# Two convolutions with group normalization: singles of both convolutions side by side, both roots taken ahead of mid's normalization, and a new order of VectorE's work

## The reference

```python
x = x + _L0_conv_ref(_gn(x), L0_conv_weight, L0_conv_threshold)   # 3x3, padding 1, weights masked by a threshold
x = x + _L1_conv_ref(_gn(x), L1_conv_kernel, L1_conv_bias)        # 5x5 by FFT, which is a 5x5 convolution with padding 2, plus bias

def _gn(v, G=16, eps=1e-05):          # groups of 2 channels over the whole image
    g = v.reshape(B_, G, C_ // G, H_, W_)
    m = jnp.mean(g, axis=(2, 3, 4), keepdims=True)
    s = jnp.var(g, axis=(2, 3, 4), keepdims=True)
    return ((g - m) / jnp.sqrt(s + eps)).reshape(v.shape)
```

## Time and profile before

| | |
|---|---|
| median of 3 executions | 901.29 us (901.25 to 901.67) |
| the profiled execution | 901.0 us, of which its span is 899.2 us |
| mean granted TensorE clock | 0.955 |
| busy: PE, PE weight loads, DVE, ACT, POOL | 88%, 57%, 68%, 37%, 26% of the span |
| DMA | 150.59 MB, mean 167 GB/s |

### The profile page before, as it was taken

The page is one execution under the profiler, slowest core; times in us unless marked ns, Lnnn a source line. Parts: engine busy times, 40 slices in busy tenths (PEclk is TensorE's granted clock), DMA queues, the critical chain, the costliest instruction groups (busy, mean ns, idle before and its releaser), DMA issues.

```text
span 899.2 us, 67768 instructions
## 1 busy us (share of the span) xinstructions
PE 794.9 (88%) x32302; PEld 508.1 (57%) x32302; DVE 611.0 (68%) x949; ACT 336.1 (37%) x289; POOL 234.5 (26%) x165
## 2 busy tenths in 40 slices
PE   0785698989899898989899898989899898997895
PEld 0342365656567565756566575656566565664463
DVE  6676398786767697676767687686767585664141
ACT  0342234353524244353524244353524244352320
POOL 1014042322303232321303232321303232333031
PEclk9887999999999999999999999999999999999898
DMA  8989875978788686878888676978886554664313
GB/s 182 207 178 227 172 154 141 210 171 204 182 191 209 156 181 161 192 181 194 189 196 197 148 186 163 210 181 192 191 197 163 131 134 113 148 156 97 72 47 93
DMA packets 234118, 150.59 MB, mean 167 GB/s; under 512 B 18592, under 2 KB 227552, under 8 KB 229984
## 3 DMA queue, kind: packets, MB, share of 16 engines
q1 hardware_dynamic: 228768, 144.67, 70.3%
q10 hardware_dynamic: 4608, 4.23, 1.9%
q0 software_dynamic: 704, 1.25, 0.6%
HBM read 75.60 MB, written 33.59 MB: 121 GB/s over the span
## 4 chain that ended last, share of the span: by engine, by line
PE 75%; DVE 8%; issue 7%; ACT 4%; DVEq 2%; DMA 1%; POOL 1%; SPq 1%; ACTq 0%; POOLq 0%
PE psum L773 56%; PE psum L791 19%; ACT x_hi L379 3%; DVE mid L651 2%; DVEq L654 2%; DMA x_bands<-x_dram 1%; DVE bn_out L659 1%; DVE bn_in L560 1%; DVE x_lo L631 1%; ACT root L372 0%; SPq L251 0%; DVE x_lo L639 0%; DVE rinv L607 0%; DVE newton L609 0%; DVE newton L608 0%
## 5 line engine op out<-in xcount | busy, mean ns | idle before, releaser
L360 POOL TENSOR_TENSOR mid<-mid,conv_out 128x512 f32<-128x512 f32 x122 | 216.8, 1806 | 598.4 <-ACT conv_out L424 598.4
L773 PE MATMUL psum<-x_hi,s_hi 32*64 32x512 f16 x6656 | 211.8, 399 | 47.6 <-DVEq L654 37.8
L773 PE MATMUL psum<-x_hi,s_lo 32*64 32x512 f16 x6656 | 206.9, 391 | 1.9 <-issue 1.9
L773 PE MATMUL psum<-x_lo,s_hi 32*64 32x512 f16 x6656 | 200.7, 381 | 2.6 <-issue 2.6
L773 PEld LDWEIGHTS psum<-x_hi,s_hi 32*64 32x64 f16 x6656 | 107.1, 107 | 137.9 <-DVEq L654 44.6
L773 PEld LDWEIGHTS psum<-x_hi,s_lo 32*64 32x64 f16 x6656 | 126.9, 109 | 72.6 <-issue 16.0
L379 ACT ACTIVATE x_hi<-x_bands 128x2304 f16<-128x2304 f32 x32 | 68.0, 2126 | 265.4 <-PE psum L791 262.4
L651 DVE SCALAR_TENSOR_TENSOR mid<-psum,unscale,x_own 128x1024 f32<-128x1024 f32 x64 | 79.2, 1279 | 127.0 <-PE psum L791 126.5
L773 PEld LDWEIGHTS psum<-x_lo,s_hi 32*64 32x64 f16 x6656 | 111.7, 104 | 76.0 <-issue 13.9
L424 ACT ACTIVATE conv_out<-psum,bias,unscale 128x512 f32<-128x512 f32 x122 | 85.1, 777 | 61.4 <-PE psum L773 38.5
L639 DVE TENSOR_TENSOR x_lo<-mid_bands,x_hi 128x2560 f16<-128x2560 f32 x32 | 99.0, 3094 | 0.8 <-PE psum L773 0.5
(11 more groups left out here) (77 smaller groups left out, 267.9 us busy)
## 6 DMA issues: line engine op xcount, KB each, us to landing
x_own<-x_dram SPq DMA_DIRECT2D x128, 256.0 KB, 5.0
mid_bands<-mid SPq DMA_DIRECT2D x372, 80.0 KB, 2.1
out_dram<-mid SPq DMA_DIRECT2D x116, 256.0 KB, 5.5
x_bands<-x_dram SPq DMA_DIRECT2D x96, 288.0 KB, 6.1
x_bands<-x_dram SPq DMA_DIRECT2D x32, 272.0 KB, 6.4
mid_bands<-mid SPq DMA_DIRECT2D x124, 64.0 KB, 2.0
every_mv<-mv_scratch ACTq DMA_DIRECT2D x16, 256.0 KB, 3.7
out_dram<-mid SPq DMA_DIRECT2D x24, 128.0 KB, 2.4
```

Source lines behind the costliest of these rows:

```text
L360: nc.gpsimd.tensor_tensor(m, m, conv_out[:, b, :], ALU.add).then_inc(out_added, 1)
L773: ins = nc.tensor.matmul(psum[2 * C * J:2 * C * (J + 1), bank + i, :].rearrange("p (a w) -> p a w", a=A), w[quad(i), at:at + 2, :].rearran ...
```

## The change

TensorE: the helpers are cut anew. A whole step now does `pairs3_high` (96 pairs on `x3_hi`), `pairs3_low` (48 pairs on `x3_lo`), `pairs5_high` (320 pairs on `x5_hi`), `singles3` (96 singles on `x3_hi`, then 48 on `x3_lo`), `singles5` (80 singles on `x5_lo`, then 160 on `x5_hi`), `pairs5_low` (160 pairs on `x5_lo`). The number of products is as before. Two semaphores change: `high3_whole` is raised when `x3_hi` has been read for the last time, and `high3` waits for it instead of `c3_whole`; `a5_whole` now is raised after the last read of `x5_hi`, and `high5` waits for it instead of `b5_begun`, which is gone. `x3_lo` is now needed after 96 matmuls of a step, and the 5x5 banks and `x5_hi` after 144.

ScalarE: in even steps both roots are taken one after the other, ahead of `normalize5`.

VectorE: a whole step now does `low5`, `normalize3(s+1)`, (even steps) both `group_stats`, both `scale_of`, (odd steps) `stats_in` of halves s+3 and s+4, then `take_conv3`, `stats_out`, `aggregate`, and at the end `low3(s+1)` for the next step. In the lead the bound of the 5x5 weights (`largest`, `power_of_two`, for which POOL's split of these weights waits) is taken ahead of `take_conv3(1)` instead of after the statistics of mid, `low3(2)` stands ahead of `stats_out(0)`, and `take_conv3(2)` ahead of `mean_of(("mid", 0))`. TensorE's start of the lead becomes a block of its own, placed behind `lead_warm`, with a branch to it and one back.

```diff
--- before.py
+++ after.py
@@ -142,7 +142,7 @@
 
         c3_whole = sem("c3_whole")
         a5_whole = sem("a5_whole")
-        b5_begun = sem("b5_begun")
+        high3_whole = sem("high3_whole")
         b5_whole = sem("b5_whole")
         mean_mixed = sem("mean_mixed")
         var_mixed = sem("var_mixed")
@@ -375,7 +375,7 @@
 
                 act.wait_ge(norm1, h + 1)
                 if h:
-                    act.wait_ge(c3_whole, h)
+                    act.wait_ge(high3_whole, h)
                 nc.scalar.activation(x3_hi[:, :, 2:2 + W], x_bands[:, h % XB_SLOTS, :, :], ACT.Copy).then_inc(hi3_done, 1)
                 act.drain().then_inc(x3_hi_go, 1)
 
@@ -383,7 +383,7 @@
 
                 act.wait_ge(norm2, k + 1)
                 if k:
-                    act.wait_ge(b5_begun, k)
+                    act.wait_ge(a5_whole, k)
                 nc.scalar.activation(x5_hi[:, :, 2:2 + W], mid_bands[:, k % MB_SLOTS, :, :], ACT.Copy).then_inc(hi5_done, 1)
 
             def scale_by(which, v):
@@ -457,7 +457,8 @@
                     spread_stats(s - 1)
                 if gathered:
                     gather_stats(s - 1)
-                    take_root(gathered[0])
+                    for stat in gathered:
+                        take_root(stat)
                 if s == 0:
                     high3(1)
                     take_root(("x", 1))
@@ -477,8 +478,6 @@
                         high3(s + 1)
                     if has5(s + 1):
                         high5(s + 1 - LAG)
-                if len(gathered) > 1:
-                    take_root(gathered[1])
                 if exchanged(s) and s >= LAG:
                     spread_stats(s)
 
@@ -694,24 +693,24 @@
             low3(1)
             variance_of(("x", 1))
             scale_of(("x", 1))
-            take_conv3(1)
-            stats_out(0)
-            low3(2)
-            stats_out(1)
-            aggregate("mid", 0, mean_go)
             dve.wait_ge(w_loaded, 16 * 2 * Q)
             largest(w5, 1)
             power_of_two(1)
             nc.vector.drain().then_inc(w5_bounded, 1)
+            take_conv3(1)
+            low3(2)
+            stats_out(0)
+            stats_out(1)
+            aggregate("mid", 0, mean_go)
+            take_conv3(2)
             mean_of(("mid", 0))
-            take_conv3(2)
             variance_of(("mid", 0))
             scale_of(("mid", 0))
-
             low3(LAG)
             stats_in(4, range(BANKS))
             stats_in(5, range(BANKS))
             aggregate("x", 2, mv_ready)
+
             low5(0)
             stats_out(2)
             dve.wait_ge(mix_loaded, 16)
@@ -719,13 +718,13 @@
             group_stats(("x", 2))
             scale_of(("x", 2))
             normalize3(LAG + 1)
+            take_conv3(LAG)
             stats_in(6, range(BANKS))
-            take_conv3(LAG)
+            stats_in(7, range(BANKS))
             stats_out(LAG)
-            stats_in(7, range(BANKS))
             aggregate("mid", LAG // 2)
             aggregate("x", (LAG + 3) // 2, mv_ready)
-            stats_in(8, range(BANKS))
+            low3(LAG + 1)
 
             for s in range(LAG + 1, STEPS):
                 gathered = exchanged(s - 1)
@@ -734,20 +733,18 @@
                 low5(s - LAG)
                 if s > HALVES:
                     add_late(s - 1 - LAG)
-                if has3(s):
-                    low3(s)
+                if has3(s + 1):
+                    normalize3(s + 1)
                 if gathered:
                     dve.wait_ge(mv_in, 16 * exchange_number(s - 1))
-                    group_stats(gathered[0])
-                    scale_of(gathered[0])
-                if has3(s + 1):
-                    normalize3(s + 1)
-                if len(gathered) > 1:
-                    group_stats(gathered[1])
-                if has3(s + 5):
-                    stats_in(s + 5, range(BANKS))
-                if len(gathered) > 1:
-                    scale_of(gathered[1])
+                for stat in gathered:
+                    group_stats(stat)
+                for stat in gathered:
+                    scale_of(stat)
+                if s % 2:
+                    for h in (s + 3, s + 4):
+                        if has3(h):
+                            stats_in(h, range(BANKS))
                 if has3(s):
                     take_conv3(s)
                     stats_out(s)
@@ -755,6 +752,8 @@
                     aggregate("mid", s // 2, None if len(exchanged(s)) > 1 else mv_ready)
                     if len(exchanged(s)) > 1:
                         aggregate("x", (s + 3) // 2, mv_ready)
+                if has3(s + 1):
+                    low3(s + 1)
 
             take_late(HALVES - 1)
             add_late(HALVES - 1)
@@ -794,33 +793,39 @@
                                 start=start and dx == 0, stop=True, skip_group_check=True, tile_position=(i * C, j * C))
                 return ins
 
-            def high_image3():
+            def pairs3_high():
 
                 pe.wait_ge(bank3_go, 1)
                 pe.wait_ge(x3_hi_go, 1)
                 pairs(s3_hi, x3_hi, K3, X3_BANK, start=True, every=x3_hi_go)
                 pairs(s3_lo, x3_hi, K3, X3_BANK, every=bank3_go)
-                singles(s3_hi, x3_hi, K3, X3_BANK)
-                singles(s3_lo, x3_hi, K3, X3_BANK)
-
-            def low_image3():
+
+            def pairs3_low():
 
                 pe.wait_ge(x3_lo_go, 1)
                 pairs(s3_hi, x3_lo, K3, X3_BANK, every=x3_lo_go)
+
+            def singles3():
+
+                singles(s3_hi, x3_hi, K3, X3_BANK)
+                singles(s3_lo, x3_hi, K3, X3_BANK).then_inc(high3_whole, 1)
                 singles(s3_hi, x3_lo, K3, X3_BANK).then_inc(c3_whole, 1)
 
-            def high_image5():
+            def pairs5_high():
 
                 pe.wait_ge(x5_hi_go, 1)
-                singles(s5_hi, x5_hi, K5, X5_BANK, start=True)
-                singles(s5_lo, x5_hi, K5, X5_BANK)
-                pairs(s5_hi, x5_hi, K5, X5_BANK, every=x5_hi_go)
-                pairs(s5_lo, x5_hi, K5, X5_BANK).then_inc(a5_whole, 1)
-
-            def low_image5(step):
+                pairs(s5_hi, x5_hi, K5, X5_BANK, start=True, every=x5_hi_go)
+                pairs(s5_lo, x5_hi, K5, X5_BANK)
+
+            def singles5():
 
                 pe.wait_ge(x5_lo_go, 1)
-                singles(s5_hi, x5_lo, K5, X5_BANK).then_inc(b5_begun, 1)
+                singles(s5_hi, x5_lo, K5, X5_BANK)
+                singles(s5_hi, x5_hi, K5, X5_BANK)
+                singles(s5_lo, x5_hi, K5, X5_BANK).then_inc(a5_whole, 1)
+
+            def pairs5_low(step):
+
                 pe.reg_add(step, step, 1)
                 pairs(s5_hi, x5_lo, K5, X5_BANK, every=x5_lo_go).then_inc(b5_whole, 1)
 
@@ -843,23 +848,19 @@
 
             pe.wait_ge(warm_set, 1)
             pe.wait_ge(mix_loaded, 16)
-            mix_mean(("x", 0))
-            mix_variance(("x", 0))
-            keep_warm(16)
-            pe.wait_ge(w3_go, 1)
-
             only = [pe.engine]
             step = pe.alloc_register("step")
             pe.reg_mov(step, 0)
-            pe.br("lead_high")
+            pe.br("lead_start")
             with nc.body("lead_high", valid_engines=only):
-                high_image3()
+                pairs3_high()
                 pe.br_eq(step, 1, on_true="lead_variance", on_false="lead_low")
             with nc.body("lead_variance", valid_engines=only):
                 mix_variance(("x", 1))
                 pe.br("lead_low")
             with nc.body("lead_low", valid_engines=only):
-                low_image3()
+                pairs3_low()
+                singles3()
                 pe.reg_add(step, step, 1)
                 pe.br_eq(step, 1, on_true="lead_mean", on_false="lead_later")
             with nc.body("lead_mean", valid_engines=only):
@@ -871,10 +872,17 @@
             with nc.body("lead_warm", valid_engines=only):
                 keep_warm(8)
                 pe.br("lead_high")
+            with nc.body("lead_start", valid_engines=only):
+                mix_mean(("x", 0))
+                mix_variance(("x", 0))
+                keep_warm(16)
+                pe.wait_ge(w3_go, 1)
+                pe.br("lead_high")
             with nc.body("lead_mid", valid_engines=only):
                 mix_mean(("mid", 0))
                 mix_variance(("mid", 0))
                 keep_warm(6)
+                pe.br("lead_end")
             nc.switch_bb("lead_end")
             pe.wait_ge(w5_split, 3)
 
@@ -882,16 +890,19 @@
             pe.br("whole_step")
             with nc.body("whole_step", valid_engines=only):
                 hint = pe.mark_branch_hint_location()
-                high_image3()
-                high_image5()
-                low_image3()
-                low_image5(step)
+                pairs3_high()
+                pairs3_low()
+                pairs5_high()
+                singles3()
+                singles5()
+                pairs5_low(step)
```

(5 more changed lines are left out.)

## The result

The changed kernel takes 836.01 us (median of 4, 834.83 to 836.88) against 901.48 of the kernel before (also a median of 4; the 901.29 above is one of three), a ratio of 0.9268 (95% interval 0.9251 to 0.9286). The forecast was 832 with 820 to 864. The profiled execution took 834.8 with a span of 833.0, and its mean granted clock is 0.980 against 0.955. First the page of the changed kernel, to be held against the earlier trace rows: PE is busy for 91% of a shorter span, and the low parts of x take 2.5 us on the mean instead of 3.1: in the kernel before those beside POOL's additions took 3.6 (475.63, with POOL at work from 474.30 to 482.98) and the others 2.5 (453.44), and now in the loop none runs beside them.

What follows compares the result with a forecast made beforehand. PE was taken to be bound by its own pace plus 2.78 us waits for the 3x3 banks and the clock drops behind them. Gains of 36.1 + 17.6 + 12.2 + 3.0 = 68.9 us from 901.3 gave 832, range 820 to 864.

Steps and rivals of the forecast that it cites:

- The waits and drops: Step ends: 13 PE waits for the 3x3 banks and 11 clock drops go, gaining 36.1 and 17.6 us.
- Singles side by side: TensorE's steps: two shape changes instead of four save 0.38 us in each of 32 steps, 12.2 us.
- The lead: Before the loop: earlier weights' bound and new orders; with the first pass, taken as -3 us.
- Rival F: Branch to or from lead_start: an instruction fetch makes the lead longer, 839 us; chance 0.08.
- The first pass: Loop's first pass: PE's 17.0 us of unexplained waits read as instructions not yet loaded; reordering bounds +6.8 to -6.8 us.
- No new wait: Within the steps: later needs stay covered, smallest spare 0.9 us before the 5x5 banks; costed at nothing.
- A: First 5x5 pair: ScalarE late, so the 5x5 banks become PE's wait, clock may drop, 868 us; chance 0.09.
- B: Loading: SP or the DMA engines hold the step, 861 us; chance 0.07.
- C: Step boundaries: the waits go but clock drops stay in most pairs of steps, 850 us; chance 0.08.
- D: PE before pairs3_low: x3_lo late from VectorE's queue, slower at 978 us; chance 0.05.

Runs made afterwards that it cites:

- e3: The kernel before with one ScalarE edit alone, both roots taken ahead of mid's normalization in even steps: 844.02 us, ratio 0.9357.
- e2: The changed kernel with the 3x3 singles put between 3x3 and 5x5 pairs, so four shape changes a step again: 844.98 us, ratio 0.9371.
- e1: The changed kernel with TensorE's start of the lead back in line ahead of the loop blocks: 831.06 us, ratio 0.9206.
- e6: e1 with VectorE's lead in the old order again: 831.95 us, ratio 0.9233.
- e7: e1 with two loads (x_own of half 4, x_bands of half 8) moved behind the normalization of half 4: 831.59 us, ratio 0.9233.
- e8: e1 with three loads (x_own of half 4, x_bands of halves 8 and 9) held until the loop's first pass is over: 823.78 us, ratio 0.9137.
- e5: The changed kernel with two extra ScalarE copies (1.1 us) before the 5x5 banks are released, steps 4 to 31: 838.69 us, ratio 0.9301.
- e4: The changed kernel with the second root (x's) taken after high5 again, VectorE's new order kept: 908.43 us, ratio 1.0081.

## Why the prediction was right, point by point

- *The waits and drops* (36.1 + 17.6 = 53.7): the mechanism held as drawn, and e3 shows it by itself, with 57.5 us by the medians. In the traces step 4 to step 31 take 682.8 us in the kernel before and 628.9 in e3, 53.9 less, as forecast; the rest of the 57.5 lies in the lead and the last steps (1.7 us) and in the spread of the runs. The rival that the old order of VectorE would keep part of the wait fell.
- *Singles side by side* (12.2): over-sized. e2 gives 9.0 at the end for the 29 passes of the loop, 0.34 us for one change in and out; at that price the three last steps, which e2 leaves as they are, would add 1.0 (an estimate from e2). The term had been taken above its direct reading (0.31) towards what was left of a step; that rest belongs to something else that no run here separates.
- *The lead* (-3): wrong in sign, in two steps. The first was to let the wait for the first statistics cover the branch to `lead_start`. Rival F, which had a chance of 0.08, is what happened there, on the way to the block. e1 shows the price, 5 us, of 6.6 at the first product. The sentence of the Trainium skill ("Runtime: NRT & Kernel Launch", Instruction fetch mechanics), that such a branch must first fetch its target, agrees with this trace: PE had nothing to issue until 26.4 although its input was there at 19.8, and a transfer of 16 KB of instructions landed at 24.8. The second was to take a gain in the lead as one that lasts. In e1, without the branch, step 3 starts 4.6 us earlier than in the kernel before (65.45 against 70.08) and step 4 only 0.8 us (116.39 against 117.20), since the first pass got 3.8 us longer. e6 shows that VectorE's new lead order gives nothing behind the first pass.
- *The first pass*, read as instructions not yet loaded: right, as the transfers on queue 8 show, 7 in the first pass and none in the later ones. The forecast left out that they share the DMA engines with the kernel's own traffic. e7 and e8 move nothing but SP's loads, and e8 shortens the pass from 51.0 to 42.0 us. In the kernel before the pass took 47.1 us at a DMA share of 0.87 and a clock of 0.86, in the changed kernel 49.9 at 1.02 and 0.80 (windows below, before and after); that the fuller engines made it longer fits e8, but no run tests it for this pair. In e8 the DMA engines stand nearly idle from 90 to 101 and the blocks still come 3.7 us apart, so a part is not contention.

```profile
70.10:117.20 47.10, 30.06 (x1008) 16.74 (x1016) 26.16 (x45) 12.76 (x8) 8.41 (x15) 0.86 0.87 180
69.70:119.60 49.90, 31.84 (x1014) 17.24 (x1021) 28.38 (x47) 12.77 (x8) 0.00 (x0) 0.80 1.02 207
```

- *No new wait* (0): right. Spare before the 5x5 banks 0.9 forecast, 1.0 by e5; spare of `x_lo` at the end of an even step 1.8 forecast, 2.6 here (`low3` done at 461.8, its pairs start at 464.4), and 2.0 at the end of an odd one. Rivals A, B, C and D did not come. B was the least far away: SP waited 30.4 us for POOL's additions, where it had waited 3.7, and the DMA share rose to 0.93, more than the 0.87 worked out from bytes.
- Together: 57.5 for the roots, 9.0 for the shapes, -5.0 for the block of the lead's start leave 4 of the 65.5 us. They are not in the lead: step 4 starts at 116.66 in e3 and at 116.39 in e1. From there to step 31 e3 takes 12.9 us more than e1, of which the shapes are 9.1 (e2 against the changed kernel); the other 3.8 are mostly in e3's steps 4 to 6 (25.2, 23.6 and 23.7 us), and no run says which part of the new orders removes them. Of 68.9 forecast, 65.5 came. The lead fell short by 5.4 and the shapes by up to 3.2, and what came in besides, among it the 4 us that no term had, made up for more than half of that. So the forecast total is nearer than its parts deserve, which is luck.

## What to carry to other kernels

When an engine in order holds a one-element operation (here a square root of 0.2 us) behind long ones, follow the waits across both queues: its place decided 57 of 65 us, and the same new orders without it would have won nothing (e4). Write out the next-late event with its spare before moving work; here 0.9 us for the 5x5 banks was right to 0.1, and the part of a delay beyond it cost its own length. TensorE code that is run for the first time was paced here by its own loading, which the profile lists among the DMA queues: look there when an engine waits for `issue`, keep the first block in line, and keep bulk loads that nobody needs yet out of the first pass.

## What the runs showed of the hardware

- A branch ahead, over some 600 instructions, kept TensorE without work until 26.4 us with the DMA engines full (share 1.00 from 10 us on); in line its first product started at 19.8. The 16 KB of instructions that it waited for were transferred from 23.45 to 24.81.
- In the first pass of a loop of 2016 products and weight loads TensorE waited at points 128 products apart, 8.4 us from one to the next with the DMA engines full (79.52 to 87.94 in e7), and 3.7 us with them nearly idle (e8). Each wait with the cause `issue` in the changed kernel's first pass ended 1.4 to 1.7 us behind the landing of a 16 KB transfer of instructions. Later passes show no such wait and no such transfer.
- A change of the products' shape from 32x32 to 32x64 and back costs 0.34 us (e2), 0.22 of it on the way to the wider one.
- A 2.78 us gap of TensorE was followed by a drop of the granted clock in 11 of 13 cases (the step behind it took 24.7 to 24.9 us), at 1.6 us each, and not in the two that ended at 143.6 and 549.7 (23.2 us). In e5, where each step was 0.1 us longer at the first 5x5 pairs, the clock stayed at 2.4 GHz (1.00).
- A VectorE subtraction with both inputs in SBUF took 3.6 us beside a GpSimd addition and 2.5 without one (475.63 and 453.44 in the kernel before).
